# Attention's rows of twenty tiles: turned through DRAM and VectorE's 32x32 transposes, not by TensorE

## What is computed

```python
qp = jax.nn.elu(q) + 1.0
kp = jax.nn.elu(k) + 1.0
kv = jnp.einsum('bhsd,bhse->bhde', kp, v)
z = jnp.einsum('bhsd,bhd->bhs', qp, kp.sum(axis=2))[..., None]
attn = jnp.einsum('bhsd,bhde->bhse', qp, kv) / (z + EPS)
out = attn.transpose(0, 2, 1, 3).reshape(b, s, HID)
return out @ o_w.T + o_b
```

## Time and profile before

| | us |
|---|---|
| median of 3 runs | 2030.18 (2029.66 to 2031.02) |
| the profiled execution: its own time | 2035.76 |
| its span in the trace | 2034.2 |
| PE busy in the span | 1991.9 |
| DVE busy | 907.2 |
| ACT busy | 627.6 |
| POOL busy | 441.4 |

### The profile page before, as it was taken

The page is one execution under the profiler, slowest core; times in us unless marked ns, Lnnn a source line. Parts: engine busy times, 40 slices in busy tenths (PEclk is TensorE's granted clock), DMA queues, the critical chain, the costliest instruction groups (busy, mean ns, idle before and its releaser), DMA issues. The chain is left out here.

```text
span 2034.2 us, 29845 instructions
## 1 busy us (share of the span) xinstructions
PE 1991.9 (98%) x10606; PEld 1763.4 (87%) x10607; DVE 907.2 (45%) x1730; ACT 627.6 (31%) x981; POOL 441.4 (22%) x545
## 2 busy tenths in 40 slices
PE   9999999999999989999999999999999999999996
PEld 8899998988889889998988788889988988988995
DVE  5455575658533543345333423343235244334332
ACT  4443333335312422233222312332224224223221
POOL 2122224265621122012102111021021121120221
PEclk9999999999999999999999999999999999999998
DMA  7211223147222421053104302331044043142221
GB/s 188 70 53 63 83 73 80 53 114 230 63 42 52 144 58 26 18 158 93 21 21 130 103 21 52 114 88 21 21 124 108 21 114 108 31 106 96 52 42 21
DMA packets 115407, 156.12 MB, mean 77 GB/s; under 512 B 28560, under 2 KB 61456, under 8 KB 115344
## 3 DMA queue, kind: packets, MB, share of 16 engines
q1 hardware_dynamic: 93744, 112.13, 17.8%
q0 software_dynamic: 21600, 43.16, 11.4%
HBM read 113.16 MB, written 42.10 MB: 76 GB/s over the span
## 5 line engine op out<-in xcount | busy, mean ns | idle before, releaser
L997 DVE CAST h_hi<-h 128x512 fp32r<-128x512 f32 x320 | 139.5, 436 | 848.0 <-ACT h L741 824.5
L577 POOL DMA_INDIRECT out_dram<-ys,tab_s x80 | 128.5, 1607 | 1008.4 <-DVE ys L990 990.1
L1445 PE MATMUL bank<-w_hi,h_hi 128*128 128x512 f32 x752 | 296.4, 394 | 0.0
L1448 PE MATMUL bank<-w_lo,h_hi 128*128 128x512 f32 x752 | 295.0, 392 | 0.0
L1449 PE MATMUL bank<-w_hi,h_lo 128*128 128x512 f32 x752 | 295.0, 392 | 0.0
L741 ACT ACTIVATE h<-bank,b_cur 128x512 f32<-128x512 f32 x160 | 110.0, 688 | 532.3 <-PE bank L1449 520.8
L741 ACT ACTIVATE h<-pair_v,b_cur 128x512 f32<-128x512 f32 x160 | 110.1, 688 | 494.7 <-PE pair_v L1449 490.8
L1445 PE MATMUL bank<-et_hi,w_hi 128*128 128x384 f32 (+1 forms) x640 | 229.1, 358 | 9.4 <-issue 9.4
L1449 PE MATMUL bank<-et_hi,w_lo 128*128 128x384 f32 (+1 forms) x640 | 228.6, 357 | 0.0
L1448 PE MATMUL bank<-et_lo,w_hi 128*128 128x384 f32 (+1 forms) x640 | 228.1, 356 | 0.0
L1449 PE MATMUL pair_v<-et_hi,w_lo 128*128 128x384 f32 (+1 forms) x640 | 227.6, 356 | 0.0
(11 more groups left out here) (259 smaller groups left out, 3558.5 us busy)
## 6 DMA issues: line engine op xcount, KB each, us to landing
w_raw<-L_ffn_w_dram SPq DMA_DIRECT2D x128, 512.0 KB, 3.8
xb<-_attn_hidden_states_dram SPq DMA_DIRECT2D x32, 256.0 KB, 2.7
xr<-_attn_hidden_states_dram SPq DMA_DIRECT2D x32, 256.0 KB, 3.3
out_dram<-x SPq DMA_DIRECT2D x32, 256.0 KB
normed<-x1n SPq DMA_DIRECT2D x32, 256.0 KB
normed<-zrow SPq DMA_DIRECT2D x1, 2048.0 KB, 8.4
out_dram<-zrow SPq DMA_DIRECT2D x1, 2048.0 KB, 14.4
b_cur<-L_ffn_b_dram SPq DMA_DIRECT2D x8, 256.0 KB
```

The source lines that it names most:

```text
L577: nc.gpsimd.indirect_dma_start(out=out, out_offset=bass.IndirectOffsetOnAxis(ap=tab_s[:, h, 0:1].bitcast(I32), axis=0), in_=ys[:, h, :], i ...
L997: ve_.tensor_copy(h_hi[:, mm % 4, :], h32[:, mm % 2, :]).then_inc(h_split_hi, 1)
L1445: ins = mm_(out_, lh, rh, start=(first and c == 0), stop=False, skip_group_check=shared)
L1448: mm_(out_, lh, rl, start=False, stop=False, skip_group_check=shared)
```

## The change

The attention rows of tiles 0 to 19 (`A_QUADS = 20`) no longer pass through PE. In the step in which DVE writes `at`, SP sends it to DRAM (`send_a`) as four blocks, one for each quarter of the features, in pieces of 512 bytes, and reads the buffer back (`return_a`) in rows of 2 KB, so that partition 32b+q holds features 128b to 128b+127 of four tokens. One step later DVE turns the sixteen 32x32 blocks with one transpose instruction into the new tile `a32`, reading and writing with a step of four elements. ACT and DVE then take `at_hi` and `at_lo` from `a32` instead of bank 7, and later in their lists than before. Chunk k of the turned rows now holds features 4p+k instead of 128k+p, so the output weights are loaded by rows 4p+k (`BY_FOURS`), and tiles 20 to 31, which PE still turns, are read with a step of four elements (`chunk`). The warming matmuls at the start go from 14 to 2.

```diff
+            def send_a(v):
+                sp.wait_ge(at_done, v + 1)
+                sp.dma_start(a_quads[v].rearrange("(b p r) -> p b r", b=QUADS, p=P),
+                             at[:, v % 2, :].rearrange("p (b r) -> p b r", b=QUADS)).then_inc(a_sent, 16)
+            def return_a(v):
+                sp.wait_ge(a_sent, 16 * (v + 1))
+                sp.dma_start(at[:, v % 2, :], a_quads[v].rearrange("(p d) -> p d", p=P)).then_inc(a_back, 16)
...
             for t in range(1, STEPS):
+                if t - NUM in range(0, A_QUADS):
+                    send_a(t - NUM)
...
+                if t - NUM in range(0, A_QUADS):
+                    return_a(t - NUM)
...
+            def quads_turned(dst, src):
+                return ve_.transpose(dst.rearrange("p (k i a) -> p k a i", k=KC, a=QUADS),
+                                     src.rearrange("p (a j k) -> p k a j", a=QUADS, k=KC))
...
-                if v >= 2:
-                    dve.wait_ge(att_full, v - 1)
+                if v >= A_QUADS + 2:
+                    dve.wait_ge(att_full, v - A_QUADS - 1)
...
-                if v is not None:
-                    dve.wait_ge(att_hi_done, v + 1)
-                    split_lo(bank[7], at_lo[:, v % 2], at_hi[:, v % 2], att_lo_done)
+                if v is not None and v < A_QUADS:
+                    a_rows_turned(v)
...
-            warm(14, 1)
+            warm(2, 1)
...
-                if v is not None:
+                if v is not None and v >= A_QUADS:
                     pe.wait_ge(at_done, v + 1)
-                    if v >= 1:
-                        pe.wait_ge(att_lo_done, v)
-                    turn(bank[7], at[:, v % 2, :]).then_inc(att_full, 1)
+                    pe.wait_ge(att_lo_done, v)
+                    turn(bank[7], at[:, v % 2, :], True).then_inc(att_full, 1)
```

More of the change, by code:

```diff
@@ L52, in moe_block @@
     RRING = 3
+    QUADS = 4
     QSLOTS = 3
@@ L59, in moe_block @@
     normed_t = normed[0:T, :].rearrange("(b t p) d -> b t p d", b=B, p=P)
+    a_quads = nc.dram_tensor("a_quads", [NTILES, QUADS * P * P], F32).ap()
     table = nc.dram_tensor("slot_table", [SLOTS + PAD_SLOTS, 2], F32).ap()
@@ L123, in moe_block @@
         at = sa("at", [P, 2, D])
+        a32 = sa("a32", [P, D])
         at_hi = sa("at_hi", [P, 2, KC, P], F32R)
@@ L192, in moe_block @@
         xt_full, xt_hi_done, xt_lo_done = n_("xt_full"), n_("xt_hi_done"), n_("xt_lo_done")
+        a_sent, a_back = n_("a_sent"), n_("a_back")
+        a_turned = n_("a_turned")
         att_full, att_hi_done, att_lo_done = n_("att_full"), n_("att_hi_done"), n_("att_lo_done")
@@ L237, in moe_block @@
         MATRICES = "vkqo"
+        BY_FOURS = "o"
+        A_QUADS = 20
         MATRIX_STEPS = (2, 2, 5, 8)
@@ L291, in turn_bank, with chunk @@
             return bank[(5, 6, 7, 5)[c]]
+        def chunk(row, k):
+            return row.rearrange("p (i k) -> p k i", k=KC)[:, k]
         def q_slot(half):
@@ L779, in tile_end, with a_hi @@
                     w2_split(e + 1, 7)
+            def a_hi(src, v):
+                if v >= 2:
+                    act.wait_ge(o_full, v - 1)
+                split_hi(src, at_hi[:, v % 2], att_hi_done)
             def gate_turned(c):
@@ L840, in _ @@
                 v = tile_at(t, TURN_A)
-                if v is not None:
-                    act.wait_ge(att_full, v + 1)
-                    if v >= 2:
-                        act.wait_ge(o_full, v - 1)
-                    split_hi(bank[7], at_hi[:, v % 2], att_hi_done)
+                if v is not None and v >= A_QUADS:
+                    act.wait_ge(att_full, v - A_QUADS + 1)
+                    a_hi(bank[7], v)
                 for lag, tiles in ((OUT + 1, range(0, FRESH)), (OUT + 2, range(FRESH, NTILES))):
@@ L862, in _ @@
                     nc.scalar.activation(ke[:], ke[:], ACT.Exp, scale=-1.0).then_inc(ke_done, 1)
+                v = tile_at(t, TURN_A)
+                if v is not None and v < A_QUADS:
+                    act.wait_ge(a_turned, v + 1)
+                    a_hi(a32, v)
                 r = tile_at(t, QUERY)
@@ L1145, in attention, with a_lo, a_rows_turned @@
                 ins.then_inc(at_done, 1)
+            def a_lo(src, v):
+                dve.wait_ge(att_hi_done, v + 1)
+                split_lo(src, at_lo[:, v % 2], at_hi[:, v % 2], att_lo_done)
+            def a_rows_turned(v):
+                dve.wait_ge(a_back, 16 * (v + 1))
+                quads_turned(a32[:], at[:, v % 2, :]).then_inc(a_turned, 1)
             PARTS = (6, 6, 8, 6, 6)
@@ L1290, in _ @@
                 v = tile_at(t, TURN_A)
-                if v is not None:
-                    dve.wait_ge(att_hi_done, v + 1)
-                    split_lo(bank[7], at_lo[:, v % 2], at_hi[:, v % 2], att_lo_done)
+                if v is not None and v < A_QUADS:
+                    a_rows_turned(v)
+                if v is not None and v >= A_QUADS:
+                    a_lo(bank[7], v)
                 v = tile_at(t, OUT)
@@ L1302, in _ @@
                     keys_mapped(v)
+                v = tile_at(t, TURN_A)
+                if v is not None and v < A_QUADS:
+                    a_lo(a32, v)
                 v = tile_at(t, NUM)
@@ L1450, in product, with turn @@
                 return ins
-            def turn(dst, src):
+            def turn(dst, src, by_fours=False):
                 for c in range(KC):
-                    ins = nc.tensor.transpose(dst[:, P * c:P * (c + 1)], src[:, P * c:P * (c + 1)], ident[:])
+                    ins = nc.tensor.transpose(dst[:, P * c:P * (c + 1)],
+                                              chunk(src, c) if by_fours else src[:, P * c:P * (c + 1)], ident[:])
                 return ins
```

5 lines of the change are left out of this document (3 added, 2 removed).

## The result

| | median us (lowest to highest) | runs |
|---|---|---|
| before | 2031.45 (2028.56 to 2035.14) | 20 |
| changed | 2027.82 (2025.05 to 2029.71) | 20 |

The ratio is 0.998, with a 95% interval of 0.9974 to 0.9986: 3.6 us less. The time lies in the stated range, 2018.6 to 2029.2. The profiled execution of the changed kernel took 2027.08 us, its span 2025.4. That is 8.8 us under the span of before, but the profiled execution of before lay 4.3 us over its median and this one 0.7 under its own, so the two traces alone mislead. Further on, each kernel is traced again.

A forecast was written before the change was run, and what follows sets the result against it. PE, busy 98% of the span and gapless in full steps, was taken as the bound; 8.7 us of removed turns less 0.3 (step 25) and 0.4 (step 27) gave 8.0, so 2022.2 us, range 2018.6 to 2029.2.

The forecast's parts named there:

- DVE's new order: DVE's list behind kt: transpose (taken as 0.69 us), statistics, kp, at_lo; zi starts 0.15 us earlier than before.
- step 27: x starts 4.42 us late, PE idles 1.23 us; 0.4 us lost if fixed, another 1.2 to 1.4 won if gone.
- The tail: Steps 34 to 43, where PE waits for POOL's gathers; the forecast's sum has no term for it.
- The removed turns: PE's transposes of 20 tiles at 0.434 us each leave its list with nothing in their place: 8.7 us gained.
- d = -0.15 to +0.45: Shift in us of DVE's work behind kt, judged by zi's start; +0.45 if the transpose takes 1.23 us.
- the dear transpose: DVE's transpose at 1.23 us because its step of four elements costs something; total gain then 6.2 us.
- Steps 20 and 28: Behind `state`, xn's margin of 0.29 us becomes 0.01, or a 0.59 wait; between 0 and 1.2 us for both.
- Step 25: Behind the routing, PE waits for qp; if a slow 1.09 us operation recurs, loss of 0.28 us, or 0.88.
- The way through DRAM: SP's sending and return of the attention rows costs nothing, as DVE asks for them 9.3 us later.
- the bad case: DRAM trip with the return behind the whole burst of loads: 8 us, still 1.3 us to spare.
- The strided reads of PE: PE's turns of tiles 20 to 31 with a step of four: 0 to 5.2 us, taken as nothing.
- Warming matmuls: The twelve removed at the start stood ahead of a wait for the constants ending at 3.68: nothing.

The follow-up runs named there:

- b_noturn: Kernel before without PE's turns of tiles 1 to 19, nothing in their place, output wrong; steps 13 to 33 took 282.4 us, whole time says nothing.
- a_runs: Changed kernel with features in another order, so DVE's transpose and PE's turns have no step of four elements; 2023.98 us, ratio 0.9961.
- a_warm14: Changed kernel with 14 one-column warming matmuls at the start instead of 2; 2026.49 us in one run.
- b_split: Kernel before with POOL's four early gathers moved from step 38 to two each in steps 39 and 40; ratio 1.0015.
- b_v2: Kernel before with POOL's four early gathers two each in steps 38 and 39, their rows turned in steps 42 and 44; ratio 0.9993.
- a_runs_v3: a_runs plus one early gather in each of steps 38 to 41, their rows turned in 43 and 44; ratio 0.9942.
- a_v3lo: Changed kernel with one early gather in each of steps 38 to 41 and DVE's at_lo of tiles 0 to 19 behind normalize_x; 2022.01 us, ratio 0.9953.

## Why the forecast was wrong, point by point

The forecast was 8.7 - 0.3 - 0.4 = 8.0 us. Two terms of it failed. The loss by DVE's new order was put at 0.3 us, with 0.4 more for step 27, and steps 13 to 33 lost 8.7 - 6.6 = 2.1. The tail was put at nothing, without a look at it, and took about 2.8. Together that is 8.7 - 2.1 - 2.8 = 3.8, against 3.6 measured. For the first the experiments show the cause; for the second they show only where it arises.

- **The removed turns**: the price of 0.434 us each, 8.7 in all, was right. Full steps take 13.51 to 13.54 us instead of 13.95, and in b_noturn nineteen turns less with nothing in their place give 8.8 us, 8.2 of them by this price.
- **DVE's new order** is the first step that failed. The bounds for the transpose were 0.54 and 1.23 us, and I took 0.69, "the row of the same size at the usual rate". It took 1.18. The rate I took is that of a plain transpose (0.70). With it (a_runs) steps 13 to 33 take 2.3 us less than in the changed kernel; 0.7 of that is the meeting with POOL that step 24 is spared, and 1.6 is what the step of four elements costs there. The place of zi came out within the forecast d = -0.15 to +0.45, at +0.06, but by luck: for a transpose of 1.18 us the working gives +0.40, and for a_runs' 0.70 it gives -0.14 where -0.34 was measured. It left out, for one, that each operation starts some 0.08 us before the end of the one ahead. And a shift of -0.94 was to be had (b_noturn), because at_hi without a turn ahead of it comes early; I measured the gain from before instead. My own sum with the dear transpose, 6.2 us, is near what steps 13 to 33 gave (6.6), but its terms were not those measured, as the next points show.
- **Steps 20 and 28** (19 and 27 in the table): I looked at the margin of xn's turn (0.29) and found it just enough. PE asks for kvb before that, with no margin, and waits 0.33 and 0.29 us. Put at 0, the two steps cost 0.9.
- **Step 25** (24 in the table): a loss of 0.3 was forecast, and it was 0.7; an operation drawn out by 1 us came again, as POOL's addition to xr came again beside it. **Step 33** (32) has the same chain for the next batch, and was missing in the list: 0.3 to 0.5.
- **Step 27** (26 in the table): the late wake-up was chance. The 0.4 us set aside for it did not arise.
- **The way through DRAM**: right, 6.6 us and hidden, against 8 for the bad case.
- **The strided reads of PE**: the turn and what follows go from 0.434 to 0.470 us, so 12 x 0.04 = 0.4 us, near the "nothing" I took. The Trainium skill (SBUF — State Buffer, Door 1: The DMA port swizzle), with its penalty for such steps, is borne out for DVE (0.49 us on 0.70) and all but absent on PE. The Trainium skill's figures for the transpose paths (VectorE: DVE Perf Modes, The three transpose paths) are for bf16; the estimate from them of 1.24 us is near the strided 1.18 and too high for the plain 0.70.
- **The tail** is the second step that failed: no step of the forecast looked at POOL's list in steps 34 to 41. Three traces of the changed kernel (67.9, 66.6, and 67.8 with a_warm14) lie 2.8 us in the mean above four of before (64.1, 65.7, and 63.6 and 64.9 with two warming matmuls), and 6.6 - 2.8 = 3.8 is about what was measured. In these tails PE idles 9.7, 7.0 and 10.0 us against 6.9, 8.0, 5.6 and 7.9, and more of them runs at the lower clock (10.2, 10.2 and 6.8 us against 3.4, 6.8, 6.8 and 3.4). Why the changed kernel's tail is longer stays open. All its traces are of the second kind, but the strided transpose can't be the whole cause, as b_noturn, b_split and b_v2 are of that kind without any transpose on DVE. Open is also why scatters issued 0.5 us earlier land later.
- **Warming matmuls**: "nothing" was right for the start and by luck for the rest.

The best kernel measured is a_runs_v3: 2020.17 us against 2032.57, ratio 0.9942 (0.9928 to 0.9956).

## What to carry to other kernels

Work taken off the busiest engine is worth its full time only where the chains that this engine waits for become shorter by as much. To see what the replacement costs, compare with the kernel in which the work is left out and nothing is put in its place, not with the kernel before. For an instruction that no row shows, look first for a row with a like access pattern: here that bound (1.23 us) was near the measured 1.18, and the row of the same size (0.69) was not. After a gain, look for the next list that runs in order and is not yet busy: here POOL's, in which scatters, a table load and gathers stand ahead of small operations that everyone waits for.

## What the hardware showed that was not expected

- A transpose of sixteen 32x32 f32 blocks takes 0.70 us on DVE, and 1.18 with a step of four elements on both sides.
- DVE operations with two SBUF inputs that meet POOL's addition to xr are held until it ends: 1.25 us instead of 0.23, 1.71 instead of 0.18. Which operation is hit changes with a shift of half a microsecond, so that a faster list can make a step longer (a_v3lo, step 25).
- Leaving out twelve one-column matmuls at the start of PE's program made the kernel before some 30 us slower, by waits between experts with 32 more packets of code loaded.
